# Grouped-query attention on one Trainium2 core: the order of VectorE's work in a slot

## The reference

```python
q = (hidden_states @ Wq).reshape(b, s, NH, HD)      # 32 heads of 128; k and v have 4
k = ...; v = ...
q = _rms_norm(q, q_norm_w)
k = _rms_norm(k, k_norm_w)
q, k = _apply_rope(q, k, cos, sin)                  # q * cos + rotate_half(q) * sin
k = jnp.repeat(k, groups, axis=1)
v = jnp.repeat(v, groups, axis=1)
scores = jnp.einsum('bhqd,bhkd->bhqk', q, k) * scaling
scores = jnp.where(causal[None, None], scores, jnp.finfo(scores.dtype).min)
attn = jax.nn.softmax(scores.astype(jnp.float32), axis=-1).astype(q.dtype)
out = jnp.einsum('bhqk,bhkd->bhqd', attn, v)
return out.reshape(b, s, NH * HD) @ Wo
```

## Time and profile before

| | us |
|---|---|
| median of 3 runs | 1947.77 (1946.73 to 1949.39) |
| profiled execution | 1948.34 |
| its span | 1946.4 |
| PE busy, whole span | 1556.5 (80%) |
| DVE busy | 1264.2 (65%) |
| ACT busy | 931.6 (48%) |
| POOL busy | 658.9 (34%) |

### The profile page before, as it was taken

One profiled execution on the slowest core, in us unless ns is written; L12 is line 12 of the kernel. 1 busy time (PEld: TensorE's weight loads), 2 busy tenths in 40 slices (PEclk: granted clock), 3 DMA queues, 4 the chain that ended last, 5 costly groups with the idle time before them and its releaser, 6 DMA issues. The chain is left out here.

```text
span 1946.4 us, 28135 instructions
## 1 busy us (share of the span) xinstructions
PE 1556.5 (80%) x9150; PEld 1214.7 (62%) x9158; DVE 1264.2 (65%) x2128; ACT 931.6 (48%) x2281; POOL 658.9 (34%) x671
## 2 busy tenths in 40 slices
PE   6899789779864565382769999999999999998373
PEld 4444578668851222272648888888888888886262
DVE  4665354665466998544737777777777777775533
ACT  2365344234424331252536666666666666664341
POOL 3011260415057674704832222222222222220703
PEclk9899799888987888586879999999999999999586
DMA  3321333213420000444000000000000000000443
GB/s 75 53 50 45 115 101 125 76 50 112 127 61 0 0 1 21 153 142 135 25 0 12 1 23 1 23 1 23 1 23 1 23 1 12 1 1 1 163 142 103
DMA packets 75322, 98.28 MB, mean 50 GB/s; under 512 B 11168, under 2 KB 58912, under 8 KB 75184
## 3 DMA queue, kind: packets, MB, share of 16 engines
q1 hardware_dynamic: 69040, 79.71, 13.9%
q0 software_dynamic: 6144, 16.79, 2.7%
HBM read 62.38 MB, written 27.66 MB: 46 GB/s over the span
## 5 line engine op out<-in xcount | busy, mean ns | idle before, releaser
L1226 DVE TENSOR_REDUCE gqa_neg_max<-acc 128x1 f32<-128x1024 f32 (+7 forms) x256 | 192.9, 754 | 175.6 <-PE acc L1335 174.4
L1112 ACT ACTIVATE gqa_probsT_high<-aux 128x512 fp32r<-128x512 f32 x288 | 172.0, 597 | 249.9 <-PE aux L1343 249.1
L1231 DVE TENSOR_TENSOR gqa_probsT_low<-aux,gqa_probsT_high 128x512 fp32r<-128x512 f32 x288 | 197.6, 686 | 29.8 <-ACT gqa_probsT_high L1112 25.5
L1121 ACT ACTIVATE gqa_probs<-acc,gqa_neg_max 128x1024 f32<-128x1024 f32 (+7 forms) x256 | 189.3, 740 | 29.8 <-DVE gqa_neg_max L1226 24.8
L1343 PE MATMUL aux<-ident,gqa_probs 128*128 128x128 f32 x1152 | 174.3, 274 | 0.0
L1354 PE MATMUL aux<-gqa_probsT_high,gqa_v_high 128*128 128x512 f32 x288 | 146.5, 509 | 1.0 <-DVE gqa_probsT_low L1231 1.0
L1019 POOL TENSOR_SCALAR gqa_q_scale<-gqa_q_scale 128x4 f32<-128x4 f32 x64 | 16.3, 255 | 383.4 <-ACT gqa_square L1056 383.1
L1366 PE MATMUL aux<-gqa_wo,gqa_oT 128*128 128x256 f32 x512 | 132.3, 381 | 4.4 <-DVE stream L1219 3.4
L1333 PE MATMUL acc<-gqa_k_low,gqa_q_high 128*128 128x512 f32 (+5 forms) x384 | 132.3, 345 | 0.0
L1333 PE MATMUL acc<-gqa_k_high,gqa_q_low 128*128 128x512 f32 (+5 forms) x384 | 132.0, 344 | 0.0
L1333 PE MATMUL acc<-gqa_k_high,gqa_q_high 128*128 128x512 f32 (+5 forms) x384 | 130.6, 340 | 1.6 <-DVE gqa_k_low L1181 1.6
(11 more groups left out here) (397 smaller groups left out, 4452.4 us busy)
## 6 DMA issues: line engine op xcount, KB each, us to landing
f_w<-in_f_up SPq DMA_DIRECT2D x64, 256.0 KB, 2.7
f_xs<-tokens_by_slot SPq DMA_DIRECT2D x108, 128.0 KB, 2.1
outputs_by_slot<-f_y_tile SPq DMA_DIRECT2D x108, 128.0 KB, 1.7
f_w<-in_f_down SPq DMA_DIRECT2D x64, 128.0 KB, 3.0
mat_qk<-mat_high SPq DMA_DIRECT2D x64, 64.0 KB, 2.3
gqa_w_q<-in_g_wq SPq DMA_DIRECT2D x8, 512.0 KB, 3.6
gqa_wo<-in_g_wo SPq DMA_DIRECT2D x8, 512.0 KB, 3.8
tokens_by_slot<-zeros SPq DMA_DIRECT2D x1, 3968.0 KB, 13.2
```

Of the source, the lines that this page charges most:

```text
L1112: act.activation(probsT_high[:, u % RING, :], aux[:, u % 2, :], ACT.Copy).then_inc(cell_high_ready, 1)
L1121: act.activation(out, scores(n), ACT.Exp, bias=neg_max[:, j % (2 * JOBS):j % (2 * JOBS) + 1], accum_out=row_sum[:, n // 2 % 4, m, n % 2:n ...
L1226: dve.tensor_reduce(neg_max[:, j % (2 * JOBS):j % (2 * JOBS) + 1], scores(n), AXY, ALU.max, negate=True).then_inc(max_ready, 1)
L1231: dve.tensor_tensor(probsT_low[:, u % RING, :], aux[:, u % 2, :], probsT_high[:, u % RING, :].bitcast(F32), ALU.subtract).then_inc(cell_lo ...
```

## The change

DVE's two calls for the query tile move up in a slot: from behind the additions and the low part of the cell to right behind the row maximum.

```diff
                     dve.tensor_reduce(neg_max[:, j % (2 * JOBS):j % (2 * JOBS) + 1], scores(n), AXY, ALU.max, negate=True).then_inc(max_ready, 1)
+                if z >= 1:
+                    n = query_tile(z - 1, "project")
+                    if n is not None:
+                        rope(n)
+                    n = query_tile(z - 1, "turn")
+                    if n is not None:
+                        take_low(n)
                 add(z - 1, 0)
                 u = z - CELLS
                 if 0 <= u < CELLS * BANDS:
...
                 add(z - 1, 1)
-                if z >= 1:
-                    n = query_tile(z - 1, "project")
-                    if n is not None:
-                        rope(n)
-                    n = query_tile(z - 1, "turn")
-                    if n is not None:
-                        take_low(n)
                 band, c = divmod(z, CELLS)
```

## The result

The changed kernel takes 1954.7 us (median of 8 runs, 1953.59 to 1958.11) against 1947.94 us for the kernel before (8 runs, 1946.14 to 1950.95): ratio 1.0036, 95% interval 1.0026 to 1.0046, slower by 5.1 to 9.0 us. The forecast was 1957.4 us.

A forecast was written before the change was run, and what follows sets the result against it. PE was taken as the bound, busy 707.60 of 715 us in most of the loop. Terms +22.3 - 10.7 - 2.0 = +9.6 us gave 1957.4 us, 0.5% slower; range 1952 to 1966.

The forecast's parts named there:

- The weighing in slot 8: PE's weighing waits for the cell's low part, pushed back by slot 7's rotation: 29 x 0.77 = 22.3 us cost.
- The reaction time: From the end of a low part to the PE matmul it alone held back: 0.06 us, from the loop's drain.
- The turn and the weighing in slot 2: The queries' turn on PE stops waiting for the rotation, now 0.6 us earlier: 10.7 us gained over bands 1 to 30.
- The low part of the queries: Slot 4's turn at 768 columns no longer waits for the query's low part: 0.29 us in 7 bands, 2.0 gained.
- Slots 3 and 5: The cell's low part ends 0.6 us later there, hidden behind PE's work; uncovered, at most 0.3 us a time.
- The sum: Cost and gains over the whole kernel: +22.3 - 10.7 - 2.0 = +9.6 us, giving 1957.4 us, 0.5% slower.
- Only the gain counts: Rival, 5%: the low part of slot 7 stays hidden, no stall in slot 8; about 1934.7 us, faster.
- The two cancel: Rival, 9%: engines catch up during slot 8's stall, so a later wait shrinks; under 4 us change, 1944 to 1951.6.
- The clock falls: Rival, 4%: stalls of about 1 us a band lower PE's granted clock to 0.98; 15 us more, 1972.
- Slower by more: Rival, 8%: the weighing's restart costs PE more than the reaction time, or slots 4 and 6 wait; up to 1968.

The follow-up runs named there:

- Slot 7 alone: Against the kernel before, only the rotation of slot 7 moves ahead of the cell's low part; slots 1, 3 and 5 stay: 1969.17 us, ratio 1.0104.
- slot 1 alone: Against the kernel before, only the rotation of slot 1 moves up: 1934.28 us, ratio 0.9925.
- low parts alone: Against the kernel before, only the low part of the queries (`take_low`, slots 3 and 5) moves up: 1945.38 us, ratio 0.9988.

## Why the prediction was right, step by step

- **The weighing in slot 8, +22.3 us.** Right in place and size. Forecast 0.97 us late at 1024 columns and 0.56 at 640; measured 0.97 and 0.57, and the 29 stalls sum to 22.4 us. The reaction time of 0.06 us, taken from a single row of the drain, held in all 29. Slot 7 alone shows it as a cause. What I left out is the 0.02 us that PE loses after each stall, 0.7 us in all.
- **The turn and the weighing in slot 2, -10.7 us.** Right. Measured 0.47, 0.52, 0.35 and 0.18 us against forecast 0.47, 0.48, 0.31 and 0.15, 11.5 us over the 30 bands; the low part does bind at 1024 columns, and elsewhere only in band 1. The size is a little short because unhindered the turn stands 0.44 and the weighing 0.36 us behind, where I took 0.45 and 0.38.
- **The low part of the queries, -2.0 us.** Right in size, with half of the cause. I took it for the order of slot 3 alone, and did not ask why only 768 columns show it. L1139 in slot 2 delays slot 3: 1.80 us beside POOL's L1027, 1.22 without. The rotation's move alone takes the delay away (slot 1 alone), the low part's move alone does too, and so does moving L1139: it needs the long subtraction and the order of slot 3 together. In the sum it counted once, so the total was not hurt; that was luck, not insight. Left out was band 1, whose turn in slot 4 gains 0.67 us by the low part's move. The sentence "POOL gets the rotation 0.6 us earlier, which nobody waits for" was wrong in effect: DVE gained 0.58 us by it, 7 times.
- **Slots 3 and 5.** Right, no weighing waits behind them (low parts alone, the changed kernel).
- **The sum.** Forecast +9.6 us on the median of 3 runs known then. In the loop: bands 2 to 29 +9.4, band 1 -0.2, band 30 and the drain -0.35, together +8.8. So the forecast's sum is 0.8 us high for the loop: both gains came out larger than forecast, and the 0.7 us after the stalls took back a part. The measured total is +6.8 with an interval of 5.1 to 9.0, which has the loop's +8.8 near its upper end. The 2 us between are not settled: the parts outside the loop vary more than this, and the clock in the loop's start by up to 2.8 us; whether their mean differs between the kernels, a few profiles can't tell.
- **The rivals.** "Only the gain counts" describes a kernel that can be had: it is the one with slot 7 left as it was, 17 us faster by medians (I gave -13.1 for it). "The two cancel" falls with slot 7 alone, where slot 2 still waits 1.07 us. "The clock falls" falls: the granted clock is 1.00 from band 1 on through the whole loop in every profile, past 29 stalls of up to 0.97 us. The rule of the Trainium skill that I had named with it (TensorE: Matmul & The Clock Gate, "A second HAM failure mode: psum-queue depth-cycling") has no case here. "Slower by more" falls too: the restart of the weighing costs 0.02 us, and the weighings of slots 4 and 6 don't wait.

## What to carry to other kernels

In a schedule of slots, the slack of a result is not one number: the same swap cost at most 0.15 us in three slots (the weighing of slot 2 at 1024 columns) and 0.6 to 1 us in the fourth, because the engine that waits has less work ahead of its wait there (no scores and no query work in slot 8). Before an order is changed for all slots, look for the emptiest slot of the waiting engine and compare "end of the moved work" with "arrival of the waiting engine" there, by starts in the timeline. Then make the change only where it gains: here the same edit with one condition turns +6.8 us into -17 by medians (+8.8 into -14.2 in the loop).

## What the runs showed of the hardware

- A DVE subtraction of 128x1024 with both operands in SBUF took 1.80 us where it started while a POOL multiplication on SBUF was running, and 1.21 to 1.22 us where POOL's had ended within 0.02 us or none was near, 7 instances in the loop of each kernel: 1.80 to 1.81 in the kernel before, slot 7 alone and low parts alone, 1.21 to 1.22 in the others. POOL's instruction kept its 1.04 us. In the row above, POOL's ended at 1243.70, 0.72 us after DVE's start, and DVE lost 0.59. The Trainium skill (SBUF — State Buffer, "Who interferes with whom") says that the port pair which VectorE and GpSimd share is held by one of them for its whole instruction. The rows agree in direction, and nearly in size: waiting for POOL's end and only then doing 1.22 us of work would end at 1244.92, the row ends at 1244.78, 0.14 us sooner. The same subtraction ahead of the loop (split for the first quad, at 929.18 us in the kernel before) started 1.20 us before the end of POOL's L992 and took 2.28 us: 1.20 and 1.22 make 2.42, again 0.14 more than measured.
- From the end of DVE's result to the start of the matmul that it alone held back passed 0.05 to 0.06 us, in 29 stalls. A stall on PE cost 0.02 us on top of its length.
